# An AdaLN block with a selective scan: residuals by identity products into the banks of the sums, norms and softplus without GpSimd

## The reference

```python
h = layernorm(x) * (1 + ca) + sa
x = x + ga * ssm(h)        # selective scan, 16 states, over 2048 tokens
h = layernorm(x) * (1 + cb) + sb
x = x + gb * ffn(h)        # 704 inner columns
# ssm: delta = softplus(proj(h)); B, C = proj(h)
#   state_n = exp(delta * A_n) * state_n + delta * B_n * h
#   y = sum over n of C_n * state_n  + D * h
# ffn: down(silu(gate(h) * gate_s) * (up(h) * up_s)) * down_s
```

## Time and profile before

| | us |
|---|---|
| median of 3 runs | 348.99 |
| lowest and highest | 346.91, 352.38 |
| the profiled execution | 350.55 |
| its span, first to last instruction | 348.7 |
| busy in the span: TensorE, VectorE, ScalarE, GpSimd | 258.2, 263.1, 176.0, 247.8 |
| mean granted clock of TensorE | 0.853 |

### The profile page before, as it was taken

One profiled execution on the slowest core, in us unless ns is written; L12 is line 12 of the kernel. 1 busy time (PEld: TensorE's weight loads), 2 busy tenths in 40 slices (PEclk: granted clock), 3 DMA queues, 4 the chain that ended last, 5 costly groups with the idle time before them and its releaser, 6 DMA issues.

```text
span 348.7 us, 3819 instructions
## 1 busy us (share of the span) xinstructions
PE 258.2 (74%) x1234; PEld 191.7 (55%) x1234; DVE 263.1 (75%) x361; ACT 176.0 (50%) x260; POOL 247.8 (71%) x142
## 2 busy tenths in 40 slices
PE   8760486995455679867799977648997881899996
PEld 8610373854435454644676645426675660686774
DVE  3305789899958999997998599869998977941521
ACT  1442553766444496687337366963164695302410
POOL 2016869999999999999999697997499993000000
PEclk9985576888855998895699999985999996689999
DMA  7505974643526354354344463445455300000001
GB/s 276 182 9 168 315 177 87 85 98 98 121 60 125 59 129 105 109 98 83 87 97 80 99 130 93 99 82 101 82 121 144 69 1 0 0 2 30 31 2 64
DMA packets 33174, 33.10 MB, mean 95 GB/s; under 512 B 14912, under 2 KB 20224, under 8 KB 33152
## 3 DMA queue, kind: packets, MB, share of 16 engines
q1 hardware_dynamic: 32736, 32.01, 39.7%
q10 hardware_dynamic: 416, 0.81, 0.6%
HBM read 30.40 MB, written 2.36 MB: 94 GB/s over the span
## 4 chain that ended last, share of the span: by engine, by line
DVE 32%; PE 28%; POOL 19%; issue 11%; ACT 9%; DVEq 1%; POOLq 0%; ACTq 0%
DVE state L900 17%; POOL drv L588 10%; DVE drv L881 7%; PE side L1163 7%; POOL drv L601 5%; PE sums L1208 4%; PE decay L1147 3%; PE side L1131 3%; ACT gates L744 2%; PE side L1164 2%; ACT decay L756 2%; DVE gates L864 2%; PE side L1088 2%; PE decay L1088 2%; PE decay L1029 2%
## 5 line engine op out<-in xcount | busy, mean ns | idle before, releaser
L588 POOL TENSOR_TENSOR drv<-u,brow 128x1024 f32<-128x1024 f32 x64 | 150.2, 2364 | 3.8 <-DVE state L900 3.5
L756 ACT ACTIVATE decay<-delta,A 128x512 f32<-128x512 f32 x128 | 87.8, 689 | 97.2 <-DVE state L900 94.6
L900 DVE TENSOR_TENSOR_SCAN state<-decay,last,drv 128x512 f32<-128x512 f32 x96 | 120.1, 1271 | 14.3 <-ACT decay L756 14.1
L1208 PE MATMUL sums<-ident,drv 128*128 128x128 f32 x512 | 79.0, 313 | 5.9 <-POOL drv L601 5.9
L1208 PEld LDWEIGHTS sums<-ident,drv 128*128 128x128 f32 x512 | 70.3, 164 | 18.0 <-issue 8.2
L601 POOL TENSOR_TENSOR drv<-state,crow 128x1024 f32<-128x1024 f32 x28 | 69.1, 2466 | 14.1 <-DVE state L900 13.9
L1182 PE MATMUL rows_ps<-c_parts,sel 64*128 64x512 f32 x36 | 20.8, 578 | 61.1 <-DVE drv L881 56.8
L881 DVE TENSOR_TENSOR drv<-state,rows_ps 128x512 f32<-128x512 f32 x72 | 47.6, 662 | 0.5 <-PE rows_ps L1182 0.4
L1182 PEld LDWEIGHTS rows_ps<-c_parts,sel 64*128 64x128 f32 x36 | 7.6, 211 | 72.2 <-DVE drv L881 59.4
L900 DVE TENSOR_TENSOR_SCAN state<-decay,drv 128x512 f32<-128x512 f32 x32 | 37.9, 1209 | 6.4 <-POOL drv L588 3.4
L1131 PE MATMUL side<-h_hi,ffn_hi 128*128 128x512 f32 x76 | 30.6, 489 | 8.8 <-DVE gates L853 5.9
(11 more groups left out here) (134 smaller groups left out, 301.9 us busy)
## 6 DMA issues: line engine op xcount, KB each, us to landing
brow<-bc_dram SPq DMA_DIRECT2D x32, 512.0 KB, 5.6
crow<-bc_dram SPq DMA_DIRECT2D x12, 512.0 KB, 6.4
resid<-in_x SPq DMA_DIRECT2D x4, 512.0 KB, 6.9
out<-resid SPq DMA_DIRECT2D x8, 256.0 KB, 2.3
crow<-bc_dram SPq DMA_DIRECT2D x4, 256.0 KB, 3.9
gates<-in_wmod ACTq DMA_DIRECT2D x1, 768.0 KB, 6.1
gates<-in_wmod SPq DMA_DIRECT2D x1, 768.0 KB, 7.5
last<-state SPq DMA_DIRECT2D x48, 1.0 KB, 2.2
```

The lines of the kernel that those rows point to most:

```text
L588: nc.gpsimd.tensor_tensor(drv[j % RING_DRV][:, :, 0:S], u[:, c % 2, :, 0:S], b.unsqueeze(1).to_broadcast([P, HALVES, S]), ALU.mult).then_i ...
L756: nc.scalar.activation(decay[i % RING_DECAY][:, 0:S], delta[:, c % 2, h, 0:S], ACT.Exp, scale=A[:, h * N + n:h * N + n + 1]).then_inc(deca ...
L900: nc.vector.tensor_tensor_scan(state[j % RING_STATE][:, h, 0:S], decay[i % RING_DECAY][:, 0:S], drv[j % RING_DRV][:, h, 0:S], before, ALU. ...
L1208: ins = nc.tensor.matmul(sums[:, b * D + h * P:b * D + (h + 1) * P], of[:, h, b * P:(b + 1) * P], ident[:, :], is_transpose=True, start=Fa ...
```

## The change

- `x2`: TensorE adds `resid` to `sums` by products with the identity (four of 128x256 for a chunk, in `add_dterm`), and ScalarE copies `sums` to `resid` in two halves. `out`: the same in the bank of the down projection (four products for a chunk), ScalarE copies it to `resid`. VectorE does neither any more.
- Layernorm: ScalarE makes exp(-0.5 * ln(var + eps)) (`rstd`), VectorE nmr from two operands in SBUF. GpSimd has no part in it.
- softplus: relu(z) + ln(1 + exp(-|z|)). ScalarE has one pass more for each half (`abs`), the cap goes, exp reads SBUF.
- The start: u and the first drive on VectorE, in halves, with the first B row spread by TensorE (`brow`); GpSimd begins with the second drive. The modulation product is ahead of W, bc ahead of z, `diag` is a piece of its own behind W, two of the four groups of keep-warm transposes go, the ffn weights are loaded earlier.
- Slots: the statistics for chunk 1 go far ahead, the norms half a slot or a slot later, `equal` from slot 20 to 24 (behind `wb` at 22), `hi0` and `hi1` from 18 and 20 to 21 and 23. The table load for the last silu stands behind the last xn.

The core of the diff:

```diff
@@ PLAN
     "vector": [
-        (17.5, "K hdn4"), (1.5, "K x2"), (2, "K st0"), (2.5, "K st1"), (2.5, "K agg"), (19, "K out0"), (21, "K out1"),
+        (17.5, "K hdn4"), (3, "K st0"), (3.5, "K st1"), (3.5, "K agg"), (5, "K nmr"),
...
-        (-4, "F st0"), (-3.5, "F st1"), (-3.5, "F agg"),
+        (-3, "F st0"), (-3, "F st1"), (-2.5, "F agg"), (-1, "F nmr"),
...
     "gpsimd": [
-        (4, "K rstd"), (6, "F cap"), (11, "F u"), (-2, "F rstd"),
+        (11, "F u"),
     ],
     "scalar": [
-        (-0.5, "F xn0"), (0, "F xn1"), (2.5, "F hmod0"), (3, "F hmod1"), (4.5, "F exp0"), (4.5, "F zb0"),
-        (5, "F exp1"), (5, "F zb1"), (5.5, "K xn0"), (6, "K xn1"), (7, "K hi0"), (7.5, "K hi1"), (8, "F bc"),
+        (-1.5, "F rstd"), (0, "F xn0"), (0.5, "F xn1"), (2.5, "F hmod0"), (2, "K x20"), (2.5, "K x21"), (3, "F hmod1"), (4.5, "K rstd"), (19.5, "K out0"), (21.5, "K out1"),
+        (4.5, "F abs0"), (4.5, "F zb0"), (5, "F abs1"), (5, "F zb1"), (5.5, "K xn0"), (6, "K xn1"), (6, "F exp0"),
+        (6.5, "F exp1"), (7, "K hi0"), (7.5, "K hi1"), (8, "F bc"),
...
-SECOND_LATER = 2
+SECOND_LATER = {"st0": -7, "st1": -7, "agg": -7}
@@ FIRST
     "vector": [
-        (0, "F st0"), (0, "F st1"), (0, "F agg"), (1, "S xpT"), (4, "S mod"), (4, "S W"), (7, "F clo"),
-        (8, "F delta0"), (8, "F delta1"), (18, "S mod2"), (19, "S gb"), (20, "S equal"), (22, "S wb"), (31, "S same"),
+        (0, "F st0"), (0, "F st1"), (0, "F agg"), (0, "F nmr"), (1, "S xpT"), (4, "S mod"), (4, "S W"), (5, "S diag"),
+        (6, "F clo"), (8, "F delta0"), (8, "F u0"), (8, "F drive0"), (9, "F delta1"), (9, "F u1"), (9, "F drive1"),
+        (18, "S mod2"), (19, "S gb"), (22, "S wb"), (24, "S equal"), (31, "S same"),
...
     "tensor": [
-        (0, "S warm"), (0, "S warm"), (0, "S xpT"), (0, "S warm"), (0, "S W"), (1, "S mod"), (2, "F xT"),
-        (2, "S warm"), (3, "F z"), (4, "F bc"), (5, "F sp"), (18, "S mod2"), (18, "S gb"), (21, "S wb"), (30, "S same"),
+        (0, "S warm"), (0, "S warm"), (0, "S xpT"), (0, "S mod"), (1, "S W"), (2, "F xT"),
+        (2, "F bc"), (3, "F z"), (5, "F sp"), (5, "S brow"), (18, "S mod2"), (18, "S gb"), (21, "S wb"), (30, "S same"),
@@ scalar, side_work
+                elif name[:2] == "x2":
+                    q = int(name[2:])
+                    act.wait_ge(added, upto_added(c, N - 1))
+                    nc.scalar.activation(resid[:, BLK0[c] + 2 * q:BLK0[c] + 2 * q + 2, :],
+                                         sums[:, 2 * q * D:2 * (q + 1) * D].rearrange("p (b d) -> p b d", b=2),
+                                         ACT.Copy).then_inc(x2_ready, 1)
+                elif name[:3] == "out":
+                    q = int(name[3:])
+                    src, i, k = side_bank(("K down", c, q))
+                    act.wait_ge(side_full[i], k + 1)
+                    nc.scalar.activation(resid[:, BLK0[c] + 2 * q:BLK0[c] + 2 * q + 2, :],
+                                         src[:, :].rearrange("p (b d) -> p b d", b=2), ACT.Copy)\
+                      .then_inc(side_free[i], 1)
@@ vector, side_work
+                elif name == "nmr":
+                    dve.wait_ge(rstd_ready[kind], c + 1)
+                    nc.vector.scalar_tensor_tensor(nmr[kind][:, 0:nb], meanvar[kind][:, 0:nb, 0], -1.0,
+                                                   rstd[kind][:, 0:nb], ALU.mult, ALU.mult)\
+                      .then_inc(nmr_ready[kind], 1)
@@ tensor, down
+                    pe.wait_ge(x2_ready, PAIR0[c] + b // 2 + 1)
+                    nc.tensor.matmul(to, ident[:, :], resid[:, BLK0[c] + b, :], start=True, stop=False)
                     for j in range(FULL):
-                        nc.tensor.matmul(to, gates[:, j, rows], down_sb[:, j, :], start=j == 0, stop=False)
+                        nc.tensor.matmul(to, gates[:, j, rows], down_sb[:, j, :], start=False, stop=False)
@@ tensor, add_dterm
                 if c:
-                    pe.wait_ge(x2_ready, c)
+                    pe.wait_ge(x2_ready, PAIR0[c])
+                pe.wait_ge(x_loaded[c], 16)
                 for b in range(NBLK[c]):
+                    nc.tensor.matmul(sums[:, b * D:(b + 1) * D], ident[:, :], resid[:, BLK0[c] + b, :],
+                                     start=b % 2 == 0, stop=False)
```

More of the change, by code:

```diff
@@ L20 @@
 EPS = 1e-5
-EXP_CAP = 1e17
 CHUNK = [512, 512, 512, 512]
@@ L191, in side_tasks @@
             kind, name = task.split(" ")
-            for later in (0, SECOND_LATER) if kind == "F" and plan is PLAN else (0,):
+            for later in (0, SECOND_LATER.get(name, 2)) if kind == "F" and plan is PLAN else (0,):
                 at = start + later
@@ L607, in _ @@
                     if step == 0 and slot == 0:
-                        for n in range(LEAD):
+                        for n in range(1, LEAD):
                             drive(0, n)
@@ L836, in side_work @@
                     nc.vector.scalar_tensor_tensor(delta[:, c % 2, h, 0:S], src[:, 0:S], gabs[:, h:h + 1],
-                                                   delta[:, c % 2, h, 0:S], ALU.mult, ALU.max)\
+                                                   delta[:, c % 2, h, 0:S], ALU.mult, ALU.add)\
                       .then_inc(side_free[i], 1)
+                elif name in ("u0", "u1"):
+                    h = int(name[1:])
+                    dve.wait_ge(*emptied(("F sp", c, h)))
+                    dve.wait_ge(*emptied(("F xT", c, h)))
+                    nc.vector.tensor_tensor(u[:, c % 2, h, 0:S], delta[:, c % 2, h, 0:S],
+                                            hmod[:, c % 2, h, 0:S], ALU.mult).then_inc(first_u_ready, 1)
+                elif name in ("drive0", "drive1"):
+                    h = int(name[5:])
+                    src, i, k = side_bank(("S brow", 0, 0))
+                    if h == 0:
+                        dve.wait_ge(side_full[i], k + 1)
+                    dve.wait_ge(first_u_ready, h + 1)
+                    nc.vector.tensor_tensor(drv[0][:, h, 0:S], u[:, c % 2, h, 0:S], src[:, 0:S], ALU.mult)\
+                      .then_inc(first_drive_ready if h == 0 else side_free[i], 1)
                 elif name in ("lo0", "lo1"):
@@ L955, in setup @@
                       .then_inc(mod_steps, 1)
+                    dve.wait_ge(proj_loaded, 32)
+                    for k in range(HALVES):
+                        ins = nc.vector.tensor_scalar(xbc_sb[:, k, :], xproj_sb[:, k, R:R + 2 * N], sgn[:, k:k + 1], None,
+                                                      ALU.mult)
+                    ins.then_inc(xbc_ready, 1)
+                elif name == "diag":
                     dve.wait_ge(mod_steps, 2)
@@ L1054, in setup @@
                                                start=k == 0, stop=k == HALVES - 1)
+                elif name == "brow":
+                    pe.wait_ge(*emptied(("F bc", 0, 0)))
+                    pe.wait_ge(sel_ready, 1)
+                    ins = nc.tensor.matmul(to[:, 0:CHUNK[0]], sel[:, N:N + 1].to_broadcast([2 * 2 * N, P]),
+                                           c_parts[:, 0, 0:CHUNK[0]], start=True, stop=True)
                 elif name == "xpT":
@@ L1138, in side_work @@
                     to, full = take(("K down", c, pair))
+                    pe.wait_ge(x2_ready, PAIR0[c] + pair + 1)
+                    for b in range(2):
+                        nc.tensor.matmul(to[:, b * D:(b + 1) * D], ident[:, :], resid[:, BLK0[c] + 2 * pair + b, :],
+                                         start=b == 0, stop=False)
                     for j in (FULL, *range(FULL)):
@@ L1147, in side_work @@
                             ins = nc.tensor.matmul(to[:, b * D:(b + 1) * D], gates[part, j, rows],
-                                                   down_sb[part, j, :], start=j == FULL and b == 0,
+                                                   down_sb[part, j, :], start=False,
                                                    stop=j == FULL - 1 and b == 1)
```

144 lines of the change are left out of this document (64 added, 80 removed), and 11 rows, old and new, of tables (CLOSING, FIRST, PLACE).

## The result

The changed kernel takes 353.81 us (median of 4 runs, 353.32 to 354.25), the kernel before 348.62 beside it (346.91 to 352.38): ratio 1.0165, 95% interval 1.0121 to 1.0209. It is slower by some 1.2 to 2.1%. The forecast was 358 within 344 to 365. The profiled execution took 354.25 us with a span of 352.4, 3.7 us more than the 348.7 of before.

What follows compares the result with a forecast made beforehand. VectorE was taken as the first bound, with TensorE late at wb, the second down pairs and the end. Terms -7.8 + 1.3 + 3.8 + 5.0 + 2.9 + 4.0 = +9.2 us on 350.55; against the median, 358 us, range 344 to 365.

Steps and rivals of the forecast that it cites:

- rival A: Small nmr instructions slip through the VectorE/GpSimd port without waiting, everything else as forecast: 354.2 us; chance 0.17.
- Start: Up to the first scan: earlier modulation, shorter logarithm path, VectorE's u and drive bring it to 26.3 from 34.14, -7.8 us.
- Rival D: First products run at TensorE's lower clock with fewer transposes before them, start gains 4.1 us less: 362 us; chance 0.10.
- Step 0: First scan window: decay wait of 4.17 us goes, but the comparison is uncovered (+4.1) and two norms add 2.0: +1.3 us.
- The port: VectorE's two-SBUF-input nmr waits for GpSimd's whole instruction, 1.0 us on average, at four open places: about 4 us.
- Step 1: Second scan window: ScalarE's crowded queue delays the seventh scan 2.8 us, chunk 3's norm adds 1.0: +3.8 us (0 to +6).
- Step 2: Third scan window: identity products delay TensorE's second down pair by 3.8 us, xn and exp behind it add 1.2: +5.0 us.
- Rival B: TensorE's extra passes find room in steps 2 and 3, so VectorE's saved 2.6 us count: 345 us; chance 0.15.
- Step 3: Fourth scan window: TensorE's 3.8 us minus 1.3 of order, h_hi behind it +0.6: +2.9 us (-2.6 to +5).
- The end: Behind the last scan: TensorE is alone, eight identity products add 3.8 us, ScalarE's order 0.2: +4.0 us (+3 to +5).
- Rival C: VectorE alone decides from first scan to last, with the comparison still covered: -14.4 us, 334.6 us; chance 0.10.

Runs made afterwards that it cites:

- e9: Changed kernel with the first chunk's u and first drive back on GpSimd and B's row by DMA: 358.99 us, ratio 1.024 to the kernel before.
- e8: Changed kernel without the residual part, nmr as four tensor_scalar, weights' comparison ahead of wb again: 342.33 us, ratio 0.974 to the kernel before.
- e7: Changed kernel without the residual part and with nmr as four tensor_scalar: 343.35 us, ratio 0.986 to the kernel before.
- e4: Changed kernel with nmr as four one-tensor-input tensor_scalar in place of one two-input instruction: 354.54 us, ratio 1.013 to the kernel before.
- e1: Changed kernel with only the residual part undone (no identity products, VectorE adds again): 346.17 us, ratio 0.987 to the kernel before.
- e2: Changed kernel with the identity products alone left out, residual never added, copies and waits kept: 343.22 us, ratio 0.980 to the kernel before.
- e11: Changed kernel, products kept, but VectorE instead of ScalarE copies the down projection out: 356.93 us, ratio 1.018 to the kernel before.
- e5: Changed kernel with the residual part undone for the down projection only, the sums keeping their products: 348.22 us, ratio 0.995 to the kernel before.
- e3: Changed kernel with VectorE's comparison of the weights ahead of wb again in step 0: 355.74 us, ratio 1.013 to the kernel before.

## Why the prediction was right

It was right in direction and place; its sum was 9.2 us over the kernel before where the profiled executions are 3.7 apart and the medians 5.2. The time, 353.8, lies at the lower edge of what the forecast called its own (353 to 364), nearer to rival A's 354.2 than to 358, though A's mechanism is refuted by the nmr rows; and by the classes of the prediction it is "within" (342 to 356), given 0.38, not "slower", given 0.50. So the reasons did better than the number. All parts but step 0 came out below their terms. Its steps in turn.

**Start: -7.8 forecast, -9.2 measured.** The mechanism held; e9 put 3.7 us of it on u and the drive. I took z's passes at the rates of the earlier trace rows, 5.40 us; they ran at the higher clock in 3.70. The bound of -9.5 was that case. Rival D, the lower clock, came in a milder form in the executions of other kernels: 1.8 to 2.4 us, not 4.1.

**Step 0: +1.3, measured +2.2.** The wait for wb was forecast at 6.3 us and was 5.77, the comparison forecast at 4.1 in the open and was 3.75; putting it back saved 3.7 (e8 against e7). The two norms, forecast at 2.0, took 2.31 us. The step came 0.9 us longer than the sum all the same. The forecast has no term for two waits of VectorE for decays, 0.49 and 0.42 us, that the changed step shows at 52.5 and 79.1; no run isolates them.

**The port: four times 1.0 us.** Right in kind and size. The four that were counted as open, two each in steps 0 and 1, took 1.51, 0.80, 1.63 and 0.69 us, 4.63 in all; with 0.16 for each where GpSimd was idle, 4.0 us are wait. In other kernels one such instruction took 0.50 to 2.28 us beside GpSimd. e4 gained only 1.0 us in each of the two steps because its four instructions take 0.57 us themselves: of the 4.63 us it could save some 2.3, and it saved 1.95. It doesn't measure the whole. The later ones, which I had counted as hidden or free, gave e4 no gain.

**Step 1: +3.8, measured +2.65.** Within the bounds; the two norms are 2.3 us of rows in it, 1.0 of which e4 took out. That ScalarE's crowding is the rest was argued from the queues and not tested alone. The residual part is hardly in it (e1 +0.4, e7 against e4 none).

**Step 2: +5.0, measured +4.3.** The pair's end was forecast 31.7 us behind the first scan and came at 31.5. Leaving the products out gained 2.7 us of it (e2), and of the 1.2 us for the decays behind ScalarE's copy some 0.7 are real (e2 against e1, and e11). Rival B, that the products find room, is out in steps 2 and 3, for which it was made, and nearly true in steps 0 and 1.

**Step 3: +2.9, measured +2.1.** Leaving the products out gained 3.9 us (e2), the whole of them, where I took 3.8 less 1.3 of order; so the step without them is 1.8 us shorter than before, which I hadn't counted. With VectorE's additions back in their place it is 0.5 shorter (e1).

**The end: +4.0, measured +1.7.** This term was the worst. The products cost 3.4 us by e2 and 3.6 by e5, 3.8 forecast. What I missed was the clock again: right behind the last scan the 32 transposes of the sums had taken 5.23 us in the kernel before, at a mean granted clock of 0.70, and took 3.71 here, at 1.00. TensorE's timeline in the kernel before:

```profile
304.41 5.23 PE L1208 MATMUL sums<-ident,drv 128*128 128x128 f32 x32
```

and in the changed kernel:

```profile
306.34 3.71 PE L1256 MATMUL sums<-ident,drv 128*128 128x128 f32 x32
...
335.89 1.02 PE L1180 MATMUL decay<-resid,ident 128*128 128x256 f32 x4
336.84 5.64 PE L1190 MATMUL decay<-down_sb,gates 64*128 64x256 f32 x24
342.32 1.03 PE L1180 MATMUL decay<-resid,ident 128*128 128x256 f32 x4
343.28 5.64 PE L1190 MATMUL decay<-down_sb,gates 64*128 64x256 f32 x24
```

The last downs are 56 records, as forecast, 13.2 us for the 11.21 of the earlier trace rows.

**Rival C**, VectorE alone decides (334.6 us), fell in the changed kernel for the reasons given. e8, which gives up the products and so is another kernel than C's, reached 342.3 us, with wb's wait at 1.4 us.

## What to carry to other kernels

In this kernel an addition given to TensorE cost its passes nearly in full where TensorE's result ends a wait, and next to nothing where other engines fill the step; so count it per stage, and at the end of the kernel, where every pass was in the open. Count the whole change by its parts: here a good start (9.2 us) paid for a costly residual (7.6) and a comparison moved out of its cover (3.7, of which TensorE's clock can take back a part), and separated they gave a kernel faster than both. A small VectorE instruction with two SBUF inputs beside a busy GpSimd is worth writing with one tensor input and a per-partition scalar, here 0.57 us in place of 0.7 to 1.6; but it gains only where VectorE isn't going to wait anyway, and where GpSimd is idle it costs 0.4 us more.

## What the runs showed of the hardware

- Four tensor_scalar instructions of 128x1 with a per-partition scalar operand in SBUF took 0.57 to 0.58 us at each of the places listed beside GpSimd's tensor work, where one scalar_tensor_tensor of 128x4 took 0.50 to 2.28 us (0.15 or 0.16 with GpSimd idle); the scalar operand didn't bring the wait that a second tensor input brings.
- The same instructions, with about the same idle time before them, got either level of TensorE's clock in different executions: bc in the start took 3.59 us (e5) or 1.88 (changed kernel) after 1.13 and 1.40 us of idle, with the same program up to there; z in step 1 took 6.73 (e3) or 3.67 after 2.63 us of idle, with one VectorE piece in another place before it. One such case moved a part of the profiled time by 1.8 to 2.8 us, more than several edits here are worth; only comparing part by part told them apart.
- ScalarE copied 128x512 out of PSUM in 0.60 us, VectorE added or copied it in 0.69.
